# Attention with group norm, 8 images on one core: transposes in one block per tile, or singly between 512-column products

## Chip, cores and metric

One core of a Trainium2 chip runs the whole program. The metric is the time on the device in microseconds, from the start of an execution to its end; the times below are of several executions.

## The reference

Eight images `x` of 128 channels and 32 x 32 places (1024 tokens) go through a group norm, one attention head of width 128 and an output projection, with the input added at the end:

```
h = group_norm(x, gn_w, gn_b)                  # 32 groups of 4 channels
hf = h.reshape(B, C, 1024)
q = einsum('bcn,oc->bno', hf, wq) + bq
k = einsum('bcn,oc->bon', hf, wk) + bk
v = einsum('bcn,oc->bno', hf, wv) + bv
alpha = softmax(einsum('bnc,bcm->bnm', q, k) / sqrt(C), axis=-1)
out = einsum('bnm,bmc->bnc', alpha, v)
out = einsum('bnc,oc->bon', out, wo) + bo
return out.reshape(B, C, 32, 32) + x
```

## The kernel before

The projections of q and k are folded into one matrix (`u = A h`), those of v and of the output into another, so that per image (a batch of the program) there are the logits `u^T h` and the products with v. Each matrix is held as a 16-bit high part and a 16-bit low part, and each product is made of three: high x high, high x low, low x high.

A batch has 8 query tiles of 128 tokens. Each goes through this chain, over all engines:
1. TensorE `logits` (L471, L473, L475): 6 products of 512 columns into `S[n % 2]`, 1024 logits per query.
2. VectorE `tile_max`: the row maximum (L812) and from it the bias of the exponentials (L818).
3. ScalarE `exponentials` (L670): `probs[n % 2]` and the sums of the rows. The instruction that reads the sum stands in the profile as a second one of the same line.
4. TensorE `transposes` (L535): eight 128 x 128 transposes of 32-bit data, four into the bank `pT[0]` (half 0) and four into `pT[1]` (half 1).
5. ScalarE `high_parts` (L682): the 16-bit high part of each half, `pT_hi`.
6. VectorE `low_parts` (L828): the low part of each half, `pT_lo`.
7. TensorE `values` (L498 to L500): products with v over a group of four query tiles (512 columns), 6 per iteration: iterations 4 to 7 do group 0 of the batch, iterations 0 to 3 group 1 of the batch before. The first of a group (k == 0) waits for the low parts of the group and for the bank `O` to be copied out by ScalarE (`copy_values`, L653). `last_values` does the last group of the last batch in two halves.

The order on each engine is written out by hand in that engine's `batch`; semaphores carry the counts between them. In iteration j TensorE does the logits of tile j + 1, a projection in some iterations (`project_u`, three products of 512 columns; `project_v`, products of 129 columns, L416 to L418), the products with v, and the eight transposes of tile j. ScalarE does copies (`copy_u` L634, `copy_v` L644, `copy_values`), both high parts of tile j, then the exponentials of tile j + 1; behind those of tile 3 it adds a logarithm and an exponential for the next batch's group norm (`inverse_deviation`, L658 and L660). VectorE does the maximum and the bias of tile j + 1, in some iterations a piece of the next batch's group norm (`group_spread`, `group_affine`, `normalise`, L804), and both low parts of tile j; in the first iteration and in iteration 5 also the `reciprocals` of the sums (L839, L842), which SP sends to HBM and back as rows (`inv_line`, `inv_rows`). POOL splits h, u and v in parts and makes the output from `av`, the rows and x.

The rules of step 4 are these waits, of which each stands ahead of a first transpose:

```
pe.wait_ge(exp_done, T + 1)
...
    if not first:

        pe.wait_ge(lo_done, 2 * T - 1 + half)
```

Of the kernel before, what the change touches and what calls it, by code (L numbers as in the profile page):

```python
# [5 lines left out]
def groupnorm_attention_kernel(  # L6
# [16 lines left out]

    fp32, fp16 = mybir.dt.float32, mybir.dt.float16  # L40
    ALU = mybir.AluOpType
# [4 lines left out]
    N = HH * WW  # L46
# [9 lines left out]
    VW = C + 1  # L56
    V_PARTS = [(0, 3), (3, 3), (6, 2)]
# [6 lines left out]
    with ctx:  # L64
# [53 lines left out]
        probs = sb("probs", [128, 2, N], fp32)  # L118
# [16 lines left out]

# [278 lines left out]
        def _(pe):  # L414
# [32 lines left out]
            def logits(b, p, n, first):  # L447
# [21 lines left out]
                halves = [slice(c * HALF, (c + 1) * HALF) for c in range(N // HALF)]  # L469
                for c in halves:  # L470
                    nc.tensor.matmul(s[:, c], q_hi, h_hi[:, p, c], start=True, stop=False)  # L471
                for c in halves:
                    nc.tensor.matmul(s[:, c], q_hi, h_lo[:, p, c], start=False, stop=False)  # L473
                for c in halves:
                    last = nc.tensor.matmul(s[:, c], q_lo, h_hi[:, p, c], start=False, stop=True)  # L475
                last.then_inc(qk_done, 1)

            def values(b, j, p, first_group):
# [15 lines left out]
                for m in (2 * k, 2 * k + 1):  # L494
# [3 lines left out]
                    nc.tensor.matmul(O[:, :], vh, ph, start=(m == 0), stop=False)  # L498
                    nc.tensor.matmul(O[:, :], vh, pl, start=False, stop=False)  # L499
                    last = nc.tensor.matmul(O[:, :], vl, ph, start=False, stop=(m == TILES - 1))  # L500
                last.then_inc(av_done, 1)

            def last_values(half, key_tiles):

                bank = (misc, O)[half]
                if key_tiles[0] == 0 and half == 0:

                    pe.wait_ge(v_done, NV * B)
                if key_tiles[0] == 0:

                    pe.wait_ge(lo_done, 2 * (TILES * B - GT // 2 * (1 - half)))
# [3 lines left out]
                for m in key_tiles:  # L515
# [6 lines left out]
                if key_tiles[-1] == TILES - 1:  # L522
                    done.then_inc(last_av, 1)

            def transposes(b, n, first):
                T = TILES * b + n

                pe.wait_ge(exp_done, T + 1)
                for half in range(2):
                    if not first:  # L530

                        pe.wait_ge(lo_done, 2 * T - 1 + half)
                    for t in range(GT):
# [444 lines left out]
```

## Time and profile before

| | |
|---|---|
| median of 3 runs | 269.64 us (269.6 to 270.23) |
| profiled execution, span from first to last instruction | 266.8 us |
| its own time beside the span | not given apart; its median is 2.8 us above the span |
| TensorE (PE) busy | 254.4 us, 95% |
| VectorE (DVE) busy | 220.5 us, 83% |
| ScalarE (ACT) busy | 175.1 us, 66% |
| GpSimd (POOL) busy | 166.3 us, 62% |
| granted TensorE clock | 0.999 of full |

The span is that of one execution, with the launch and the end of the program outside it. Busy time counts instructions at work, and overlapping ones once. A busy TensorE is no TensorE at its peak, since its products are pipelined: how long one holds the array is read from the distance to the next start, and not from its own length. L numbers are lines of the kernel before.

### The profile page before, as it was taken

How to read it: one execution, taken by the hardware profiler on the slowest of the kernel's cores; microseconds unless marked ns; L12 is line 12 of the kernel's file. 1: busy time of each engine (PE TensorE's matmuls, PEld its weight loads, DVE VectorE, ACT ScalarE, POOL GpSimd, SP SyncE). 2: the span in 40 equal slices, each digit the busy share in tenths (PEclk: the TensorE clock that was granted, in tenths of full speed). 3: DMA queues.
4: the chain of work that ended last, by engine and by line, in shares of the span. 5: the costliest groups of instructions: out<-in, count | busy, mean ns of one | idle time of the engine just before them, and what ended most of it. 6: DMA issues, size and time to landing. Idle time of an engine off the chain costs nothing.

```text
span 266.8 us, 4984 instructions
## 1 busy us (share of the span) xinstructions
PE 254.4 (95%) x1599; PEld 157.1 (59%) x1599; DVE 220.5 (83%) x403; ACT 175.1 (66%) x338; POOL 166.3 (62%) x182
## 2 busy tenths in 40 slices
PE   2998999999999999999999999999999999999992
PEld 1655565655566655655665566566656556665581
DVE  2779988999888897988889898988979998678752
ACT  2457766766775786667666866766677677667650
POOL 4056394726978189744979089772997359790621
PEclk9999999999999999999999999999999999999999
DMA  4202004110141102320032102320021200211033
GB/s 118 79 0 81 1 0 119 29 53 2 18 143 40 39 2 40 121 79 0 0 93 103 42 0 40 118 79 0 0 79 17 62 0 5 75 39 42 0 82 115
DMA packets 9806, 13.05 MB, mean 49 GB/s; under 512 B 3904, under 2 KB 4672, under 8 KB 9792
## 3 DMA queue, kind: packets, MB, share of 16 engines
q1 hardware_dynamic: 9504, 12.75, 16.8%
q10 hardware_dynamic: 288, 0.13, 0.2%
q8 instruction: 6, 0.10, 0.2%
q14 instruction: 8, 0.07, 0.1%
HBM read 8.65 MB, written 4.23 MB: 48 GB/s over the span
## 4 chain that ended last, share of the span: by engine, by line
PE 90%; DMA 4%; DVE 3%; ACT 1%; issue 1%; ACTq 0%; POOL 0%; DVEq 0%
PE pT L535 21%; PE S L471 10%; PE S L473 10%; PE S L475 10%; PE O L500 10%; PE O L498 10%; PE O L499 10%; PE misc L417 3%; PE misc L416 3%; PE misc L418 3%; DMA wk_sb<-in_L_conv_wk_dram 1%; DMA inv_rows<-inv_line 1%; DMA inv_line<-row_inv 1%; ACT probs L670 1%; DVE pT_lo L828 1%
## 5 line engine op out<-in xcount | busy, mean ns | idle before, releaser
L828 DVE SCALAR_TENSOR_TENSOR pT_lo<-pT,pT_hi 128x512 f16<-128x512 f32 x128 | 82.8, 683 | 22.3 <-ACT pT_hi L682 22.3
L682 ACT ACTIVATE pT_hi<-pT 128x512 f16<-128x512 f32 x128 | 69.9, 596 | 39.8 <-PE pT L535 39.3
L812 DVE TENSOR_REDUCE neg_max<-S 128x1 f32<-128x1024 f32 x64 | 77.7, 1214 | 1.4 <-PE S L475 0.7
L670 ACT ACTIVATE probs<-S,exp_bias 128x1024 f32<-128x1024 f32 x64 | 71.7, 1121 | 1.8 <-DVE exp_bias L818 1.3
L535 PE MATMUL pT<-ident,probs 128*128 128x128 f32 x512 | 67.4, 274 | 1.8 <-DVE pT_lo L828 1.3
L535 PEld LDWEIGHTS pT<-ident,probs 128*128 128x128 f32 x512 | 58.6, 141 | 14.9 <-ACT probs L670 3.6
L498 PE MATMUL O<-pT_hi,v_hi 128*128 128x512 f16 x120 | 45.5, 379 | 0.0
L499 PE MATMUL O<-pT_lo,v_hi 128*128 128x512 f16 x120 | 45.5, 379 | 0.0
L500 PE MATMUL O<-pT_hi,v_lo 128*128 128x512 f16 x120 | 45.5, 379 | 0.0
L327 POOL TENSOR_TENSOR h_hi<-h,zero 128x512 f16<-128x512 f32 x14 | 14.6, 1041 | 47.8 <-DVE h L804 47.8
L471 PE MATMUL S<-h_hi,u_hi 128*128 128x512 f16 x128 | 38.4, 382 | 0.1
L473 PE MATMUL S<-h_lo,u_hi 128*128 128x512 f16 x128 | 38.1, 379 | 0.0
L475 PE MATMUL S<-h_hi,u_lo 128*128 128x512 f16 x128 | 38.1, 379 | 0.0
L368 POOL TENSOR_TENSOR attn<-av,inv_rows 128x512 f32<-128x512 f32 x15 | 23.2, 1546 | 6.8 <-DMA inv_rows<-inv_line 6.8
L337 POOL TENSOR_TENSOR u_hi<-u,zero 128x512 f16<-128x512 f32 x15 | 15.6, 1041 | 12.4 <-ACT u L634 12.4
L473 PEld LDWEIGHTS S<-h_lo,u_hi 128*128 128x128 f16 x128 | 12.6, 98 | 15.5 <-issue 0.6
L475 PEld LDWEIGHTS S<-h_hi,u_lo 128*128 128x128 f16 x128 | 12.5, 98 | 15.1
L818 DVE TENSOR_SCALAR exp_bias<-neg_max,c_tok 128x1 f32<-128x1 f32 x64 | 17.5, 273 | 4.7 <-POOL c_tok L347 1.9
L355 POOL TENSOR_TENSOR v_lo<-v,v_hi 128x384 f16<-128x384 f32 (+1 forms) x24 | 19.4, 810 | 1.9
L352 POOL TENSOR_TENSOR v_hi<-v,zeros 128x384 f16<-128x384 f32 (+1 forms) x24 | 20.4, 849 | 0.0
L376 POOL TENSOR_TENSOR y<-attn,xres 128x512 f32<-128x512 f32 x15 | 19.0, 1269 | 2.0
L498 PEld LDWEIGHTS O<-pT_hi,v_hi 128*128 128x128 f16 x120 | 11.7, 98 | 14.3 <-DVE pT_lo L828 2.3
(119 smaller groups left out, 318.9 us busy)
## 6 DMA issues: line engine op xcount, KB each, us to landing
inv_rows<-inv_line SPq DMA_DIRECT2D x16, 256.0 KB, 3.8
out_dram<-y SPq DMA_DIRECT2D x15, 256.0 KB, 2.0
x_sb<-in_x_dram SPq DMA_DIRECT2D x7, 512.0 KB, 3.2
x_sb<-in_x_dram SPq DMA_DIRECT2D x2, 256.0 KB, 3.4
inv_line<-row_inv SPq DMA_DIRECT2D x16, 2.0 KB, 1.4
out_dram<-y SPq DMA_DIRECT2D x2, 128.0 KB, 1.9
wq_sb<-in_L_conv_wq_dram ACTq DMA_DIRECT2D x1, 64.0 KB, 3.4
wk_sb<-in_L_conv_wk_dram ACTq DMA_DIRECT2D x1, 64.0 KB, 3.8
```

Of the source, the lines that this page charges most:

```text
L368: nc.gpsimd.tensor_tensor(by_tile(attn[:, q, :]), by_tile(av[:, q, :]), inverses(q), ALU.mult).then_inc(attn_done, 1)
L471: nc.tensor.matmul(s[:, c], q_hi, h_hi[:, p, c], start=True, stop=False)
L473: nc.tensor.matmul(s[:, c], q_hi, h_lo[:, p, c], start=False, stop=False)
L475: last = nc.tensor.matmul(s[:, c], q_lo, h_hi[:, p, c], start=False, stop=True)
L498: nc.tensor.matmul(O[:, :], vh, ph, start=(m == 0), stop=False)
L499: nc.tensor.matmul(O[:, :], vh, pl, start=False, stop=False)
L500: last = nc.tensor.matmul(O[:, :], vl, ph, start=False, stop=(m == TILES - 1))
L535: last = nc.tensor.transpose(pT[half][:, t, :], probs[:, n % 2, m * 128:(m + 1) * 128], ident[:, :])
L670: nc.scalar.activation(probs[:, n % 2, :], S[n % 2][:, :], ACT.Exp, bias=exp_bias[:, p, n:n + 1], accum_out=row_sum[:, p, n:n + 1]).then_i ...
L682: nc.scalar.activation(pT_hi[:, g, half * GT:(half + 1) * GT, n % GT, :], pT[half][:, :, :], ACT.Copy, scale=P_SCALE).then_inc(hi_done, 1)
L812: nc.vector.tensor_reduce(out=neg_max[:, p, n:n + 1], in_=S[n % 2][:, :], axis=AX.X, op=ALU.max, negate=True).then_inc(max_step, 1)
L828: nc.vector.scalar_tensor_tensor(out=pT_lo[:, g, ms, n % GT, :], in0=pT[half][:, :, :], scalar=P_SCALE, in1=pT_hi[:, g, ms, n % GT, :], op ...
```

## The change

TensorE's transposes no longer stand in one block. The four of half 0 of tile j stand one by one behind the first four of the six products with v of iteration j, and the four of half 1 behind the first four of the six logits products of iteration j + 1. In the first batch, where iterations 0 to 3 have no products with v, half 0 stands alone. ScalarE and VectorE follow: iteration j begins with the high and low part of half 1 of tile j - 1 (`past`), and half 0 of tile j comes later; on ScalarE the copies of `O` moved to the start of iterations 0 and 4, and that of u behind the high part. On VectorE the group norm's affine and its first normalisation stand before both low parts. `last_values` runs whole behind all transposes. The buffer `probs` has PB = 2 tiles, as before. The arithmetic is the same.

```diff
-            def logits(b, p, n, first):
+            def transpose_one(tile, half, t):
+
+                b, n, first = tile
+                T = TILES * b + n
+                if t == 0 and half == 0:
+
+                    pe.wait_ge(exp_done, T + 1)
+                if t == 0 and not first:
+
+                    pe.wait_ge(lo_done, 2 * T - 1 + half)
+                m = half * GT + t
+                moved = nc.tensor.transpose(pT[half][:, t, :], probs[:, n % PB, m * 128:(m + 1) * 128],
+                                            ident[:, :])
+                if t == GT - 1:
+                    moved.then_inc(tr_done, 1)
+
+            def logits(b, p, n, first, tile=None):
...
+                for i in range(6):
+                    c = slice(i % 2 * HALF, (i % 2 + 1) * HALF)
+                    last = nc.tensor.matmul(s[:, c], (q_hi, q_hi, q_lo)[i // 2],
+                                            (h_hi, h_lo, h_hi)[i // 2][:, p, c], start=(i < 2), stop=(i >= 4))
+                    if tile and i < GT:
+
+                        transpose_one(tile, 1, i)
                 last.then_inc(qk_done, 1)
...
-            def values(b, j, p, first_group):
+            def values(b, j, p, first_group, tile):
...
+                    if i < GT:
+
+                        transpose_one(tile, 0, i)
                 last.then_inc(av_done, 1)
...
             def batch(b, p, first, last):
 
                 np = 1 - p
                 for j in range(TILES):
+                    tile = (b, j, first and j == 0)
+                    past = (b, j - 1, first and j == 1) if j else (None if first else (b - 1, TILES - 1, False))
                     if j < TILES - 1:
-                        logits(b, p, j + 1, first and j == 0)
+                        logits(b, p, j + 1, first and j == 0, past)
                     elif not last:
-                        logits(b + 1, np, 0, False)
+                        logits(b + 1, np, 0, False, past)
+                    else:
+                        for t in range(GT):
+                            transpose_one(past, 1, t)
...
                     if not first or j >= GT:
-                        values(b, j, p, first and j == GT)
-                    if last and j == TILES - 1:
-                        last_values(0, (0, 1))
+                        values(b, j, p, first and j == GT, tile)
+                    else:
+                        for t in range(GT):
+                            transpose_one(tile, 0, t)
...
-                    transposes(b, j, first and j == 0)
-                    if last and j == TILES - 1:
-                        last_values(0, range(2, TILES))
...
             batch(B - 1, 1, False, True)
-            last_values(1, range(TILES))
+            for t in range(GT):
+                transpose_one((B - 1, TILES - 1, False), 1, t)
+            last_values(0)
+            last_values(1)
...
             def batch(b, p, first, second, last):
                 for j in range(TILES):
-                    if j == 0:
-                        copy_u(b, 1, first)
+                    past = (b, j - 1, not first) if j else (None if first else (b - 1, TILES - 1, False))
+                    if j == 0 and not first:
+                        copy_values(b - 1, 0, second)
+                    if j == 4 and not first:
+                        copy_values(b - 1, 1, second)
+                    if past:
+                        high_part(past, 1)
...
-                    high_parts(b, p, j, not first)
+                    high_part((b, j, not first), 0)
+                    if j == 0:
+                        copy_u(b, 1, first)
+                    if j == 4:
+                        copy_v(b, 2, first)
                     if j < TILES - 1:
-                        exponentials(b, p, j + 1, first and j == 0)
+                        exponentials(b, p, j + 1, first and j + 1 < PB)
...
             def batch(b, p, r, first, second, last):
                 for j in range(TILES):
+                    past = (b, j - 1) if j else (None if first else (b - 1, TILES - 1))
...
+                    if past:
+                        low_part(past, 1)
                     if j < TILES - 1:
                         tile_max(b, p, j + 1)
...
                     if j == 3 and not last:
-                        low_parts(b, j, (0,))
                         group_affine(b + 1, 1 - p)
                         normalise(b + 1, 1 - p, 0)
-                        low_parts(b, j, (1,))
-                    else:
-                        low_parts(b, j)
+                    if j == 4 and not last:
+                        normalise(b + 1, 1 - p, 1)
+                    low_part((b, j), 0)
```

TensorE in iteration 3, before (`S0` and `S1` are the two banks of logits, here those of tile 4; `pT0` and `pT1` are the banks of half 0 and half 1; the products into `O` are those with v):

```order
L471 MATMUL S0<-h_hi,u_hi 128x512
L473 MATMUL S0<-h_lo,u_hi 128x512 x2
L475 MATMUL S0<-h_hi,u_lo 128x512 x2
L498 MATMUL O<-pT_hi,v_hi 128x512
L499 MATMUL O<-pT_lo,v_hi 128x512
L500 MATMUL O<-pT_hi,v_lo 128x512
L498 MATMUL O<-pT_hi,v_hi 128x512
L499 MATMUL O<-pT_lo,v_hi 128x512
L500 MATMUL O<-pT_hi,v_lo 128x512
...
L532 ISA [waits exp_done]
L535 MATMUL pT0<-ident,probs 128x128 [waits lo_done]
L535 MATMUL pT0<-ident,probs 128x128 x3
```

and after, in the same iteration, its end of logits and its products with v:

```order
L441 MATMUL pT1<-ident,probs 128x128
L470 MATMUL S0<-h_hi,u_lo 128x512 x2
L498 MATMUL O<-pT_hi,v_hi 128x512
...
L439 ISA [waits exp_done]
L441 MATMUL pT0<-ident,probs 128x128 [waits lo_done]
L498 MATMUL O<-pT_lo,v_hi 128x512
L441 MATMUL pT0<-ident,probs 128x128
L498 MATMUL O<-pT_hi,v_lo 128x512
L441 MATMUL pT0<-ident,probs 128x128
L498 MATMUL O<-pT_hi,v_hi 128x512
L441 MATMUL pT0<-ident,probs 128x128
L498 MATMUL O<-pT_lo,v_hi 128x512
```

The wait for the tile's exponentials stood behind all six products with v and stands now behind the first of them; half 1 has gone on to the next iteration's logits.

ScalarE, from the exponentials of tile 2 to those of tile 5, before:

```order
L670 ACTIVATE probs,row_sum<-S0,exp_bias 128x1024 [waits tr_done,bias_done]
L682 ACTIVATE pT_hi<-pT0 128x4x128 [waits tr_done]
L682 ACTIVATE pT_hi<-pT1 128x4x128 [waits tr_done]
L670 ACTIVATE probs,row_sum<-S1,exp_bias 128x1024 [waits tr_done,bias_done]
L658 ACTIVATE ln_var<-var_eps 128x1 [waits var_out]
L660 ACTIVATE rstd0<-ln_var 128x1 [waits ln_step]
L653 COPY av<-O 128x512 [waits attn_done,av_done]
L682 ACTIVATE pT_hi<-pT0 128x4x128 [waits tr_done]
L682 ACTIVATE pT_hi<-pT1 128x4x128 [waits tr_done]
L670 ACTIVATE probs,row_sum<-S0,exp_bias 128x1024 [waits tr_done,bias_done]
```

and after:

```order
L663 ACTIVATE probs,row_sum<-S0,exp_bias 128x1024 [waits tr_done,bias_done]
L675 ACTIVATE pT_hi<-pT1 128x4x128 [waits tr_done]
L675 ACTIVATE pT_hi<-pT0 128x4x128 [waits tr_done]
L663 ACTIVATE probs,row_sum<-S1,exp_bias 128x1024 [waits tr_done,bias_done]
L651 ACTIVATE ln_var<-var_eps 128x1 [waits var_out]
L653 ACTIVATE rstd0<-ln_var 128x1 [waits ln_step]
L675 ACTIVATE pT_hi<-pT1 128x4x128 [waits tr_done]
L675 ACTIVATE pT_hi<-pT0 128x4x128 [waits tr_done]
L663 ACTIVATE probs,row_sum<-S0,exp_bias 128x1024 [waits tr_done,bias_done]
L646 COPY av<-O 128x512 [waits attn_done,av_done]
L675 ACTIVATE pT_hi<-pT1 128x4x128 [waits tr_done]
```

The high part of half 1 (`pT1`) of a tile stood ahead of the next tile's exponentials and stands now behind them, and the copy of `O` behind those of tile 4.

VectorE, iteration 3, before:

```order
L812 TENSOR_REDUCE neg_max<-S0 128x1 [waits qk_done]
L818 TENSOR_SCALAR exp_bias<-neg_max,c_tok 128x1 [waits max_step]
L828 SCALAR_TENSOR_TENSOR pT_lo<-pT0,pT_hi 128x4x128 [waits hi_done]
...
L804 TENSOR_SCALAR h<-x_sb,ga,gc 128x512 [waits h_ready,affine]
L828 SCALAR_TENSOR_TENSOR pT_lo<-pT1,pT_hi 128x4x128 [waits hi_done]
L812 TENSOR_REDUCE neg_max<-S1 128x1 [waits qk_done]
```

and after:

```order
L810 TENSOR_REDUCE neg_max<-S0 128x1 [waits qk_done]
L816 TENSOR_SCALAR exp_bias<-neg_max,c_tok 128x1 [waits max_step]
...
L802 TENSOR_SCALAR h<-x_sb,ga,gc 128x512 [waits h_ready,affine]
L826 SCALAR_TENSOR_TENSOR pT_lo<-pT0,pT_hi 128x4x128 [waits hi_done]
L826 SCALAR_TENSOR_TENSOR pT_lo<-pT1,pT_hi 128x4x128 [waits hi_done]
L810 TENSOR_REDUCE neg_max<-S1 128x1 [waits qk_done]
```

The order of low parts and maxima is the same; only the normalisation has moved ahead of the low part of half 0.

## Rows read from the trace of the kernel before

**Rows 1.** The page: busy time and share of each engine, and the chain
```profile
PE 254.4 (95%) x1599; PEld 157.1 (59%) x1599; DVE 220.5 (83%) x403; ACT 175.1 (66%) x338; POOL 166.3 (62%) x182
...
PE 90%; DMA 4%; DVE 3%; ACT 1%; issue 1%; ACTq 0%; POOL 0%; DVEq 0%
```

**Rows 2.** Busy time in the window of one batch (from its header)
```profile
core 0: us, PE busy (x) PEld busy (x) DVE busy (x) ACT busy (x) POOL busy (x), PEclk, DMA share, GB/s
113.34:143.99 30.65, 30.65 (x197) 18.78 (x197) 26.58 (x49) 21.36 (x42) 21.62 (x23) 1.00 0.17 51
```

**Rows 3.** Waits: us in total, times, longest us
```profile
PEld pT L535 <- ACT probs L670: 3.6, 5, 1.1
...
PEld pT L535 <- DVE pT_lo L828: 1.9, 6, 0.5
```

**Rows 4.** Chain by time, steady batch: start us, us held, what
```profile
119.67 0.87 PE pT L535 x8
120.54 0.43 PE S L471 x2
```

**Rows 5.** Timeline of PE (start us, us, instruction), 123.2 to 123.4, 127.2 to 128.3
```profile
123.20 0.22 PE L417 MATMUL misc<-wvc_lo,h_hi 128*128 128x129 f16 x1
123.25 0.22 PE L418 MATMUL misc<-wvc_hi,h_lo 128*128 128x129 f16 x1
123.31 0.28 PE L535 MATMUL pT<-ident,probs 128*128 128x128 f32 x1
...
127.21 0.38 PE L500 MATMUL O<-pT_hi,v_lo 128*128 128x512 f16 x1
127.43 0.27 PE L535 MATMUL pT<-ident,probs 128*128 128x128 f32 x1
...
127.97 0.49 PE L535 MATMUL pT<-ident,probs 128*128 128x128 f32 x3
128.30 0.38 PE L471 MATMUL S<-h_hi,u_hi 128*128 128x512 f16 x1
```

**Rows 6.** Timeline of ACT, 118 to 129 and 254 to 256
```profile
118.60 0.21 ACT L658 ACTIVATE ln_var<-var_eps 128x1 f32<-128x1 f32 x1
118.84 0.20 ACT L660 ACTIVATE rstd<-ln_var 128x1 f32<-128x1 f32 x1
119.71 0.59 ACT L653 COPY av<-O 128x512 f32<-128x512 f32 x1 [0.66 <-PE O L500]
120.19 1.09 ACT L682 ACTIVATE pT_hi<-pT 128x512 f16<-128x512 f32 x2
...
126.41 0.69 ACT L634 ACTIVATE u<-misc,ub 128x512 f32<-128x512 f32 x1
...
128.06 1.09 ACT L682 ACTIVATE pT_hi<-pT 128x512 f16<-128x512 f32 x2 [0.97 <-PE pT L535]
...
254.82 1.12 ACT L670 ACTIVATE probs<-S,exp_bias 128x1024 f32<-128x1024 f32 x1
...
255.91 0.60 ACT L653 COPY av<-O 128x512 f32<-128x512 f32 x1
```

**Rows 7.** Timeline of DVE, 121 to 125 and 128.7
```profile
121.43 0.21 DVE L784 SCALAR_TENSOR_TENSOR newton<-rstd,var_eps 128x1 f32<-128x1 f32 x1
...
122.93 0.68 DVE L828 SCALAR_TENSOR_TENSOR pT_lo<-pT,pT_hi 128x512 f16<-128x512 f32 x1
123.53 1.21 DVE L812 TENSOR_REDUCE neg_max<-S 128x1 f32<-128x1024 f32 x1
124.78 0.27 DVE L818 TENSOR_SCALAR exp_bias<-neg_max,c_tok 128x1 f32<-128x1 f32 x1
...
128.69 0.69 DVE L828 SCALAR_TENSOR_TENSOR pT_lo<-pT,pT_hi 128x512 f16<-128x512 f32 x1 [0.22 <-ACT pT_hi L682]
```

**Rows 8.** Timeline of ACT: exponentials of tiles 0 and 1, and of batches 1 and 7
```profile
16.62 1.11 ACT L670 ACTIVATE probs<-S,exp_bias 128x1024 f32<-128x1024 f32 x1 [0.69 <-DVE exp_bias L818]
...
19.54 1.12 ACT L670 ACTIVATE probs<-S,exp_bias 128x1024 f32<-128x1024 f32 x1
...
44.26 1.13 ACT L670 ACTIVATE probs<-S,exp_bias 128x1024 f32<-128x1024 f32 x1
...
229.12 1.13 ACT L670 ACTIVATE probs<-S,exp_bias 128x1024 f32<-128x1024 f32 x1
```

**Rows 9.** Chain by time at the end of the span
```profile
256.06 0.18 DVE scaled_sum L839
...
256.47 2.48 DMA inv_line<-row_inv
...
258.97 3.45 DMA inv_rows<-inv_line
...
264.04 0.42 DVE y L950
```

**Rows 10.** Groups by line and shape: busy us, mean ns
```profile
L771 DVE SCALAR_TENSOR_TENSOR spread<-dmean,mv 128x1 f32<-128x1 f32 x8 | 6.6, 831 | 0.3
```

More of the change, by code:

```diff
@@ L468, in logits @@
                 s, q_hi, q_lo = S[n % 2], u_hi[:, p, n * 128:(n + 1) * 128], u_lo[:, p, n * 128:(n + 1) * 128]
[L469 to L475, printed above, removed]
+                for i in range(6):
[4 more added lines that the diff above has]
+                        transpose_one(tile, 1, i)
                 last.then_inc(qk_done, 1)
-            def values(b, j, p, first_group):
+            def values(b, j, p, first_group, tile):
                 q, d, g, k = group_of(b, j)
@@ L493, in values @@
                         pe.wait_ge(av_out, g)
-                for m in (2 * k, 2 * k + 1):
+                for i in range(6):
+                    m = 2 * k + i // 3
                     vh, vl = v_hi[:, pv, m, 0:C], v_lo[:, pv, m, 0:C]
@@ L497, in values, with last_values @@
                     pl = pT_lo[:, q, m, :, :].rearrange("p t n -> p (t n)")
-                    nc.tensor.matmul(O[:, :], vh, ph, start=(m == 0), stop=False)
-                    nc.tensor.matmul(O[:, :], vh, pl, start=False, stop=False)
-                    last = nc.tensor.matmul(O[:, :], vl, ph, start=False, stop=(m == TILES - 1))
+                    last = nc.tensor.matmul(O[:, :], (vh, vh, vl)[i % 3], (ph, pl, ph)[i % 3],
+                                            start=(m == 0 and i == 0), stop=(m == TILES - 1 and i == 5))
+                    if i < GT:
+                        transpose_one(tile, 0, i)
                 last.then_inc(av_done, 1)
-            def last_values(half, key_tiles):
+            def last_values(half):
                 bank = (misc, O)[half]
-                if key_tiles[0] == 0 and half == 0:
+                if half == 0:
                     pe.wait_ge(v_done, NV * B)
-                if key_tiles[0] == 0:
-                    pe.wait_ge(lo_done, 2 * (TILES * B - GT // 2 * (1 - half)))
+                    pe.wait_ge(v_out, NV * B)
+                pe.wait_ge(lo_done, 2 * (TILES * B - GT // 2 * (1 - half)))
                 if half == 1:
                     pe.wait_ge(av_out, 2 * B - 1)
-                for m in key_tiles:
+                for m in range(TILES):
                     vh, vl = v_hi[:, 1, m, 0:C], v_lo[:, 1, m, 0:C]
@@ L521, in last_values @@
                     done = nc.tensor.matmul(o, vl, ph, start=False, stop=(m == TILES - 1))
[L522 to L533, printed above, removed]
-                        m = half * GT + t
-                        last = nc.tensor.transpose(pT[half][:, t, :], probs[:, n % 2, m * 128:(m + 1) * 128],
-                                                   ident[:, :])
-                    last.then_inc(tr_done, 1)
+                done.then_inc(last_av, 1)
             def batch(b, p, first, last):
@@ L742, in _ @@
             batch(B - 1, 1, False, False, True)
+            high_part((B - 1, TILES - 1, False), 1)
+            copy_values(B - 1, 0, False)
         @block.vector
@@ L861, in batch @@
                         group_spread(b + 1, 1 - p)
-                    if j == 4 and not last:
-                        normalise(b + 1, 1 - p, 1)
                     if j == 2 and not last:
```

42 lines of the change are left out of this document (19 added, 23 removed).

## Prediction

> **What bounds the kernel now.** I read the page first, then TensorE's rows, then ScalarE's and VectorE's. The page puts TensorE at 95% of the span and at 90% of the chain that ended last; VectorE is busy 83%, ScalarE 66% [rows 1]. In a whole batch of the steady loop, between two neighbouring group means in the chain, TensorE is busy for all of the 30.65 us, VectorE for 26.58, ScalarE for 21.36 [rows 2]. So a batch lasts as long as its products and transposes. The reader should see two things in these rows: TensorE has no slack, and VectorE has only 4 us of it per batch. TensorE waited for ScalarE's exponentials and for the low parts only a few times: 3.6 and 1.9 us in all [rows 3].
>
> **Part 1: what a single transpose costs TensorE.** Before, a tile is six products of logits (0.43 us per two), six products with v, and a block of eight transposes of 0.87 us [rows 4], 0.109 each. After, the same 8 transposes and 12 products stand alternately. The pairs that the new order makes all exist already. Product, then transpose: the first transpose starts 0.216 us after the product before it, as a product after a product does. Transpose, then product: three transposes from 127.97 and the logits' product at 128.30, so the last of them holds the array 0.109 us too, although what follows is a 16-bit product whose weights load fast: behind a 129-column product the next one starts 0.056 us later, and so does even a transpose, with its 32-bit weights [rows 5]. A transpose's own record lasts 0.27 us; one of 129 columns 0.22 and one of 512 columns 0.38, so by length it streams like some 256 columns. I take 0.109 for a single transpose: 0.216 x 12 + 0.109 x 8 = 3.46 us per tile before and after, a gain of 0. The Trainium skill (TensorE: Matmul & The Clock Gate, "LDWEIGHTS (loading the stationary operand)" and "Back-to-back issue gap") says that a load of 128 columns takes 128/1.2 = 107 ns and a 128-column product warm 56 ns. By that the block is bound by its loads, and each single transpose would save some 50 ns, 27 us over 512. The rows speak against it, since the wait behind the last transpose is the same 0.109 with a fast load behind it.
> As a bound from the nearest rows, a single transpose costs between 0.056 (the 129-column product's slot) and 0.109; the other end gives TensorE 512 x 0.053 = 27 us. Part 2 says why little of that would be seen.
>
> **Part 2: ScalarE's new order closes a loop of one tile.** VectorE's order hardly changes: low part of half 0, low part of half 1, row maximum of the tile two further, its bias. ScalarE's does: the high part of half 1 of tile j stood before the exponentials of tile j+1 and stands now behind them. So: exponentials j+1, high part of (j, half 1), low part of it, maximum j+2, bias, exponentials j+2. Each waits for the one before, once per tile, whatever TensorE does. Priced from rows [rows 6, 7]:
> exponentials to the next ScalarE instruction 1.09 (254.82 to the copy at 255.91); high part 0.60 and 0.03 to the low part (128.06 to 128.69); low part to maximum 0.60 (122.93 to 123.53); maximum to bias 1.25 (123.53 to 124.78); bias 0.27; 0.03 to the exponentials. Sum 3.87 us per tile, 30.96 per batch. That alone is above TensorE's 30.65. In the kernel before, both high parts lie ahead of the exponentials, so that the same pieces close only over two tiles, and TensorE's 3.46 to 4.1 us per tile cover them.
>
> **Part 3: what else hangs in that loop**, per batch, on top of 30.96:
> - Iteration 0. The copy of O (group 0 of the batch before) now comes after the exponentials of tile 0: 0.48 to the next instruction (119.71 to 120.19 [rows 6]). The products with v of iteration 0 may only start when it has ended (0.59), at 1.09 + 0.59 + 0.04 = 1.72 after the exponentials started, where TensorE is ready at about 1.05. Then 1.73 for products and transposes, the projection of u behind them (last product 0.43 later, its end 0.39), and ScalarE's copy of u (0.69, of which about 0.59 holds ScalarE) stands ahead of the exponentials of tile 1: 1.72 + 1.73 + 0.43 + 0.39 + 0.02 + 0.59 = 4.88 instead of 3.87: +1.01.
> - Iteration 3. Logarithm and exponential of the deviation stand between exponentials 3 and the high part: about +0.39 (118.60 to the end near 119.0).
> - Iterations 3 and 4. VectorE does the normalisation (1.50 from 121.43 to 122.93 [rows 7]) now before the low part of (3, half 0), and the products with v of iteration 4 wait for that low part, because they open a new group. Low part done 2.1 after exponentials 4 start; TensorE, ready 1.9 earlier, stands. Behind it come 1.73 of products, the second piece of v (0.28 + 0.22), its copy 0.28, then exponentials 5: 2.10 + 1.73 + 0.28 + 0.22 + 0.03 + 0.28 = 4.64: +0.77. The copy of O after exponentials 4 (0.48) lies beside this.
> - Iterations 5 and 6: TensorE is late by 0.04 and 0.10, for the projections.
> Sum 30.96 + 1.01 + 0.39 + 0.77 + 0.14 = 33.27 per batch, against 30.65 to 30.96 now ([rows 8]: 184.86 us for the six from the first exponentials of batch 1 to those of batch 7, 30.81 each). 6 x 2.46 = +14.8.
>
> **First batch, last batch, end.** The first has no products with v in four iterations; its first exponentials come 2.9 us apart (16.62 and 19.54 [rows 8]). Now: 1 waits for the projection of u behind the lone transposes (19.8 instead of 19.5), then 3.87 per tile, 0.39 and 0.77 as above: batch 1 starts at 48.2 instead of 44.26 [rows 8], +3.9. The last batch has no normalisation and no next u or v: 4.88 + 3 x 3.87 + 4.35 (copy of O) + 2 x 3.87 = 28.6 to its last exponentials, before 254.82 - 229.12 = 25.70: +2.9. Behind them the end hangs on the reciprocals, two transfers and VectorE's last four instructions [rows 9]. The reciprocals stood 1.24 after the exponentials' start and now stand behind a high part and a low part: 1.09 + 0.60 + 0.03 + 0.60 = 2.32: +1.1. The last products on TensorE (48 of 256 columns, at 0.109) then end at about the same moment as the second transfer.
> Sum +14.8 + 3.9 + 2.9 + 1.1 = +22.7: span 266.8 to 289.5. The profiled execution's own time is not shown apart; between span and the median of 269.64 lie 2.8 us of start and end, which I keep. **Forecast 292.3 us.**
> The queues: SP and POOL issue the same, in the same order; POOL is busy 21.6 of 30.65 us per batch [rows 2] and gains room as batches get longer. What the last tile loses, products for (0, 1) ahead of its transposes, lies beside the transfers.
>
> **Rivals.**
> A. *The loop holds, but the extra pieces hide* (TensorE's waits are absorbed later, copies slip between). Then a batch is 30.96 plus the 0.48, 0.39 and 0.48 of ScalarE's own pieces, 32.3, and the ends cost half: +9 + 5 = about 284. For it: ScalarE has idle time. Against: each piece is in the loop by its place in the order. If single transposes also cost 0.056, the lengths 1.73 above fall to 1.51 and the two big extras shrink by 0.3 or so each: about 288.
> B. *More waits than counted*: VectorE's spread instruction has a mean of 0.83 us [rows 10] and stands before a low part that TensorE and the next low part wait for; I counted it as hidden. 0.5 to 1 us per batch: 296 to 300.
> C. *Faster, the rule's case.* Single transposes cost 0.056 and the loop turns in less than its rows: TensorE's batch is 30.65 - 3.39 = 27.3 and VectorE's 26.58, so 3.4 x 7.7 = 26 us less, 244. It decides only if the loop with its extras falls below 30.65 a batch, a turn below 3.54 us where the rows give 3.87. Nothing in the rows shortens it.
> D. *No change*: TensorE binds as before and neither side moves it, 270. It needs the turn to be 3.54 too.
>
> **How the numbers follow.** Forecast as priced, with the inner bounds of A and B (284 to 300): 0.80; the loop weaker still, 272 to 284: 0.09; above 300: 0.04; D: 0.03; C: 0.04. The likeliest value is the sum, 292. The range of 8 in 10 is 284 to 300. A measurement of this kernel tells about 0.3% from no change, 0.8 us; faster 0.04, same 0.03, slower 0.93.
>
> **What would show it.** In the changed profile: (1) single transposes with the next product 0.109 us behind (right) or 0.056 (wrong) and TensorE's busy sum per batch; (2) the exponentials 3.87 us apart in iterations 1, 2, 6, 7, with high part, low part, maximum and bias head to tail between them, and batches of about 33.3 us; (3) TensorE idle before the products with v of iterations 0 (0.7 us) and 4 (1.9 us), released by the copy of O and by a low part, and before the first transposes; (4) ScalarE and VectorE in the chain that ended last where TensorE stood with 90%. I would be wrong if the high part of half 1 started long after the exponentials ended, waiting for TensorE, or if batches were still 30.7 us.

## The result, and the profile after

| | before | after |
|---|---|---|
| median, same chip | 269.62 us (268.35 to 270.23) | 294.25 us (293.55 to 295.2) |
| ratio | | 1.0902 (1.0868 to 1.0935) |
| span of the profiled execution | 266.8 us | 291.8 us (its own time 293.55) |

The change costs 24.6 us, 9.0%. The forecast was 292.3 us, the range 284 to 300.

The page of the changed kernel, busy time and the chain that ended last, answers to [rows 1]:

```profile
PE 258.4 (89%) x1599; PEld 170.2 (58%) x1599; DVE 213.6 (73%) x403; ACT 180.3 (62%) x338; POOL 165.9 (57%) x182
...
DVE 31%; ACT 23%; PE 21%; issue 19%; DMA 3%; ACTq 1%; DVEq 0%; POOL 0%
```

TensorE fell from 90% of the chain to 21%. VectorE, ScalarE and "issue" hold most of the rest; in the loop below "issue" is mostly the inside of instructions at work, 0.90 us of the exponentials and 0.56 of the low part. No engine is busier than 89%, and none was added more than 5.2 us of work: the kernel is bound by an order of waits. The window of batch 4, between its first exponentials and those of batch 5, answers to [rows 2] (window; its us; busy time of each engine):

```profile
148.99:182.91 33.92, 31.25 (x196) 20.44 (x195) 26.07 (x50) 22.12 (x41) 21.53 (x23) 1.00 0.15 47
```

This batch takes 33.92 us (the six take 33.73 on the mean, before 30.81) where the window of [rows 2] was 30.65, and TensorE stands for 2.67 of them. The granted clock is the upper level throughout (1.00), so none of this is the clock's. The waits of the changed kernel (us in total, times, longest) answer to [rows 3]:

```profile
ACT probs L663 <- DVE exp_bias L816: 23.6, 34, 1.7
PEld O L498 <- DVE pT_lo L826: 12.0, 6, 2.0
PE O L498 <- DVE pT_lo L826: 10.9, 7, 1.8
...
PEld pT L441 <- ACT probs L663: 8.0, 7, 1.9
...
PE O L498 <- ACT av L646: 6.8, 8, 1.0
```

The exponentials wait for their bias 34 times; before they did so 3 times, for 1.3 us. The products with v wait at a low part six or seven times, with 1.6 to 2.0 us each: once per batch, at iteration 4. They wait at the copy of O once per batch, at iteration 0.

The chain by time (start us, us held, what), one turn of the loop, from the exponentials of tile 2 of batch 4 to those of tile 3:

```profile
157.93 0.04 ACT probs L663
157.97 0.90 issue
...
159.14 0.50 ACT pT_hi L675
...
159.66 0.05 DVE pT_lo L826
159.71 0.56 issue
160.26 1.23 DVE neg_max L810
...
161.61 0.28 DVE exp_bias L816
161.91 0.04 ACT probs L663
```

This is the loop of the prediction, in its order: exponentials, high part, low part, maximum, bias, exponentials, with TensorE nowhere in it. From engine to engine the work goes over within 0.03 us. In this turn 0.12 us instead of 0.03 lie between the maximum and its bias; that term comes back below.

TensorE's timeline of the same batch (start us, us, instruction): the start of the products with v of iteration 0, logits in iteration 1, and the start of iteration 4's products with v:

```profile
150.81 0.38 PE L498 MATMUL O<-pT_hi,v_hi 128*128 128x512 f16 x1 [0.96 <-ACT av L646]
151.05 0.33 PE L441 MATMUL pT<-ident,probs 128*128 128x128 f32 x1
151.21 0.38 PE L498 MATMUL O<-pT_lo,v_hi 128*128 128x512 f16 x1
...
153.26 0.38 PE L470 MATMUL S<-h_hi,u_hi 128*128 128x512 f16 x1
153.48 0.27 PE L441 MATMUL pT<-ident,probs 128*128 128x128 f32 x1
153.59 0.38 PE L470 MATMUL S<-h_hi,u_hi 128*128 128x512 f16 x1
153.80 0.27 PE L441 MATMUL pT<-ident,probs 128*128 128x128 f32 x1
...
166.12 0.59 PE L470 MATMUL S<-h_hi,u_lo 128*128 128x512 f16 x2
168.25 0.39 PE L498 MATMUL O<-pT_hi,v_hi 128*128 128x512 f16 x1 [1.54 <-DVE pT_lo L826]
```

Product to transpose 0.22, transpose to product 0.11: a single transpose holds the array as long as one in a block. In iteration 0 TensorE waited 0.96 us for the copy of O (0.67 to 0.96 over batches 1 to 7). At iteration 4 TensorE stands from about 166.55 (166.12 and two products of 0.216) to 168.25, for a low part.

### The profile page after: what moved, and what is told of

Read it like the earlier page. It is cut to its first block, busy times and chain, and to the rows that moved or that the text cites. A ratio compares the mean times of both kernels' runs of the same rounds, so it can differ in the third digit from the quotient of the medians.

```text
span 291.8 us, 4987 instructions
## 1 busy us (share of the span) xinstructions
PE 258.4 (89%) x1599; PEld 170.2 (58%) x1599; DVE 213.6 (73%) x403; ACT 180.3 (62%) x338; POOL 165.9 (57%) x182
## 4 chain that ended last, share of the span: by engine, by line
DVE 31%; ACT 23%; PE 21%; issue 19%; DMA 3%; ACTq 1%; DVEq 0%; POOL 0%
DVE neg_max L810 19%; ACT probs L663 13%; ACT pT_hi L675 8%; PE O L498 8%; DVE pT_lo L826 5%; DVE exp_bias L816 4%; PE pT L441 4%; PE S L470 3%; ACT av L646 1%; PE misc L401 1%; DMA wk_sb<-in_L_conv_wk_dram 1%; PE misc L399 1%; PE misc L400 1%; DMA inv_rows<-inv_line 1%; DVE h L802 1%
## 5 line engine op out<-in xcount | busy, mean ns | idle before, releaser
L441 PE MATMUL pT<-ident,probs 128*128 128x128 f32 x512 | 137.6, 274 | 6.4 <-ACT probs L663 4.5
L826 DVE SCALAR_TENSOR_TENSOR pT_lo<-pT,pT_hi 128x512 f16<-128x512 f32 x128 | 87.9, 688 | 59.8 <-ACT pT_hi L675 58.3
L675 ACT ACTIVATE pT_hi<-pT 128x512 f16<-128x512 f32 x128 | 76.2, 596 | 59.7 <-PE pT L441 59.6
L441 PEld LDWEIGHTS pT<-ident,probs 128*128 128x128 f32 x512 | 71.2, 140 | 27.1 <-ACT probs L663 8.0
L470 PE MATMUL S<-h_hi,u_hi 128*128 128x512 f16 x128 | 45.3, 382 | 0.1
L470 PE MATMUL S<-h_lo,u_hi 128*128 128x512 f16 x128 | 44.9, 379 | 0.0
L470 PEld LDWEIGHTS S<-h_hi,u_hi 128*128 128x128 f16 x128 | 13.7, 108 | 9.9 <-issue 0.8
```

The source lines that it names most:

```text
L441: moved = nc.tensor.transpose(pT[half][:, t, :], probs[:, n % PB, m * 128:(m + 1) * 128], ident[:, :])
L470: last = nc.tensor.matmul(s[:, c], (q_hi, q_hi, q_lo)[i // 2], (h_hi, h_lo, h_hi)[i // 2][:, p, c], start=(i < 2), stop=(i >= 4))
L675: nc.scalar.activation(pT_hi[:, g, half * GT:(half + 1) * GT, n % GT, :], pT[half][:, :, :], ACT.Copy, scale=P_SCALE).then_inc(hi_done, 1)
L826: nc.vector.scalar_tensor_tensor(out=pT_lo[:, g, ms, n % GT, :], in0=pT[half][:, :, :], scalar=P_SCALE, in1=pT_hi[:, g, ms, n % GT, :], op ...
```

## The experiments

Two questions were open: whether the loop through ScalarE is the cause, and what a single transpose costs when TensorE does bind. Medians of before in the experiments' own jobs lie at 269.75 to 269.92 us; each ratio is to before.

| run | built on | us | ratio, interval | expected |
|---|---|---|---|---|
| e1 | after | 285.69 | 1.0587 (1.0569 to 1.0605) | 279, missed |
| e2 | e1 | 286.07 | 1.0609 (1.0580 to 1.0639) | 273, missed |
| e3 | e2 | 298.97 | 1.1059 (1.1032 to 1.1087) | as e2, missed |
| e4 | before | 292.12 | 1.0820 (1.0802 to 1.0838) | 274, size missed |
| e5 | before | 277.11 | 1.0293 (1.0231 to 1.0355) | 276.6 |
| e6 | before | 282.62 | 1.0481 (1.0418 to 1.0543) | 283.6 |
| e7 | after | 279.64 | 1.0379 (1.0316 to 1.0442) | 278 |
| e8 | before | 269.36 | 1.0001 (0.9967 to 1.0034) | 268.6 |
| e9 | after | 292.08 | 1.0829 (1.0802 to 1.0856) | 292.1 |
| e10 | before | 268.73 | 0.9956 (0.9935 to 0.9977) | 268.8 |
| e11 | e1 | 279.64 | 1.0374 (1.0331 to 1.0416) | 276 |

### e4: ScalarE's new order alone, in the kernel before

```
-                    high_parts(b, p, j, not first)
+                    high_parts(b, p, j, not first, (0,))
...
-                        if j == 2 and not last:
-                            inverse_deviation(b + 1, 1 - p)
+                    high_parts(b, p, j, not first, (1,))
+                    if j == 2 and not last:
+                        inverse_deviation(b + 1, 1 - p)
```

> The kernel before with one edit on ScalarE: the high part of half 1 of tile j stands behind the exponentials of tile j+1, as in the changed kernel, and the logarithm of the deviation behind it. TensorE keeps its block of eight and VectorE its order. Loop theory: the one-tile loop of 3.87 us exists now beside TensorE's 3.46 to 4.1 us per tile; a batch lasts 31.0 (TensorE's long tiles make up for short ones) to 31.9 us (they don't): 274 us (271 to 279). If the loop isn't the cause, it stays at 269.6 within 0.8.

Measured 292.12 us. TensorE's order is that of before, with its block of eight transposes. This one edit on another engine costs 22.2 us, where the whole change costs 24.6. The page (the chain) and the waits of this run:

```profile
DVE 44%; issue 25%; ACT 18%; PE 4%; DMA 3%; POOL 3%; ACTq 1%; DVEq 1%; POOLq 0%
```
```profile
ACT probs L670 <- DVE exp_bias L819: 57.7, 61, 1.5
```

61 of 64 exponentials wait for their bias. In batches 1 and 2 the steps from tile 1 to 2, 2 to 3 and 3 to 4 are 3.89 us each, the turn of the loop. The size was missed because more of VectorE's work sits inside this loop than I had reckoned. Its timeline in iteration 0 of batch 4:

```profile
149.87 1.28 DVE L758 BATCH_NORM_STATS2 bn<-x_sb 128x6 f32<-128x512 f32 x2
151.27 1.22 DVE L813 TENSOR_REDUCE neg_max<-S 128x1 f32<-128x1024 f32 x1
152.53 0.27 DVE L819 TENSOR_SCALAR exp_bias<-neg_max,c_tok 128x1 f32<-128x1 f32 x1
...
154.64 0.69 DVE L829 SCALAR_TENSOR_TENSOR pT_lo<-pT,pT_hi 128x512 f16<-128x512 f32 x1 [0.52 <-ACT pT_hi L682]
155.25 1.21 DVE L813 TENSOR_REDUCE neg_max<-S 128x1 f32<-128x1024 f32 x1
```

Here the channel statistics of the next batch (1.28, and 0.1 to the maximum) lie between the low part and the maximum, while in iteration 1 the maximum follows its low part after 0.61: that step takes 5.2 to 5.4 us. In iteration 6 the reciprocals stand there too (0.3 us), and that step takes 4.3 to 4.5. In batches 3 to 6 nearly every turn is another 0.08 to 0.22 us longer: the exponentials start 0.12 us behind the end of their bias (152.92 in ScalarE's timeline) instead of 0.04, and every third bias 0.1 later behind its maximum; why was not tried. So the loop is shown to be ScalarE's order by itself. That it costs the same in the kernel of the change is not thereby shown: there the statistics run ahead of the low part (149.37 to 150.65, the low part at 151.20) and cost the loop nothing, and it has extras that e4 has not, so that 22.2 and 24.6 lie close in part by chance.

### e1: VectorE takes the maximum ahead of the low part

```
-                    if past:
-                        low_part(past, 1)
                     if j < TILES - 1:
                         tile_max(b, p, j + 1)
...
+                    if past:
+                        low_part(past, 1)
```

> The changed kernel with one edit on VectorE: the maximum and bias of tile j+1 stand before the low part of half 1 of tile j-1, no longer behind it. That opens the one-tile loop (exponentials, high part, low part, maximum, bias), and nothing else moves. Loop theory: batches fall from 33.7 us to TensorE's 30.7 plus two waits per batch, 0.3 us for the copy of O before iteration 0 and about 1.0 for the low part of (3, half 0) behind the normalisation; 279 us (275 to 283). Rival 1, that the placing of the transposes itself costs the time (each single transpose slower, or TensorE losing time at each turn): it stays within 2 us of 294. Rival 2, that the waits for O and for the group's low parts carry most of the loss: it stays above 287.

Measured 285.69 us: 8.6 us less than the change as it stands, where 15 were expected. The low part is out of the loop, and from tile 1 to 2, 2 to 3 and 7 to the next 0 the exponentials now come 3.45, 3.60 and 3.46 us apart. But 3 to 4 takes 3.96 to 4.06, 0 to 1 has grown from 4.92 to 5.13 and more, and 4 to 5 from 4.62 to 4.95 and more. The waits of e1 that have grown, and its timeline of TensorE (one logits group of batch 4) and VectorE:

```profile
PEld pT L441 <- DVE pT_lo L826: 27.4, 51, 2.0
```
```profile
157.39 0.38 PE L470 MATMUL S<-h_hi,u_hi 128*128 128x512 f16 x1
158.00 0.33 PE L441 MATMUL pT<-ident,probs 128*128 128x128 f32 x1 [0.23 <-DVE pT_lo L826]
158.16 0.38 PE L470 MATMUL S<-h_hi,u_hi 128*128 128x512 f16 x1
...
159.14 0.59 PE L470 MATMUL S<-h_hi,u_lo 128*128 128x512 f16 x2
```
```profile
155.72 1.22 DVE L810 TENSOR_REDUCE neg_max<-S 128x1 f32<-128x1024 f32 x1
157.07 0.27 DVE L816 TENSOR_SCALAR exp_bias<-neg_max,c_tok 128x1 f32<-128x1 f32 x1
157.26 0.68 DVE L826 SCALAR_TENSOR_TENSOR pT_lo<-pT,pT_hi 128x512 f16<-128x512 f32 x1
...
159.77 1.22 DVE L810 TENSOR_REDUCE neg_max<-S 128x1 f32<-128x1024 f32 x1 [1.17 <-PE S L470]
```

A second loop of one tile: maximum at 155.72, bias, low part of half 1 until 157.94, the first transpose behind the first logits product at 158.00 (it overwrites what the low part read), the logits' last products from 159.14, and the next maximum at 159.77: 4.05 us. It runs over TensorE and VectorE, and where the first loop takes 3.89 it hardly shows. (0.1 of the 4.05 lies between the maximum and its bias, 1.35 instead of 1.25; without that it is the 3.96 of the other batches.)

### e2: e1, and the normalisation behind the low part of half 0

```
+                    low_part((b, j), 0)
                     if j == 3 and not last:
                         group_affine(b + 1, 1 - p)
                         normalise(b + 1, 1 - p, 0)
                     if j == 4 and not last:
                         normalise(b + 1, 1 - p, 1)
-                    low_part((b, j), 0)
```

> As the run before, and in iterations 3 and 4 VectorE's normalisation stands behind the low part of half 0 instead of before it. Loop theory: the wait before the products with v of iteration 4 goes too, about 1 us for each of seven batches; 273 us (270 to 276), and TensorE is busy again for nearly all of a batch. Had the normalisation hidden anyway, it equals the run before.

Measured 286.07 us, no gain. Tile 4 to 5 became shorter (4.95 to 4.51 us in batches 1 and 2), but 5 to 6 and 6 to 7 grew, 3.90 to 4.14 and 3.97 to 4.40. The normalisation now stands ahead of the next maximum and low part, which are the second loop. Its waits grew with it, from 27.4 to 34.0 us:

```profile
PEld pT L441 <- DVE pT_lo L826: 34.0, 61, 2.0
```

### e11: e1, with half 1's transposes behind the last four logits products

```
-                    if tile and i < GT:
-                        transpose_one(tile, 1, i)
+                    if tile and i >= 6 - GT:
+                        transpose_one(tile, 1, i - 2)
```

> As e1_max_first, but the transposes of half 1 stand behind the last four of the six logits products instead of the first four. e1_max_first came out 7 us above my 279; its trace has TensorE waiting at the first transposes for low parts (27 and 10 us on its two rows) that stand behind the maximum now, a second loop of one tile: logits, maximum, low part of half 1, next logits' first transpose, about 3.96 us per turn. Here that transpose comes 0.43 us later in TensorE's own order, so that the turn is 3.53: if this loop is what held e1_max_first up, 276 us (272 to 281). If it is something else, for instance the time at the turns between products and transposes: 285 to 287.

Measured 279.64 us. The transposes now overwrite the low part's source two products (0.43 us) later in the order, so the products ahead of them need not wait. The step 3 to 4 is 3.60 instead of 3.96, and 0 to 1 is 4.92 instead of 5.13; these steps, and their like in the first and the last batch (1.2 and 1.5 us), are most of the 6 us between e1 and e11. The chain (page) and the wait of e1 in this run:

```profile
PE 76%; DVE 11%; ACT 4%; DMA 4%; issue 3%; ACTq 0%; DVEq 0%; POOL 0%
```
```profile
PEld pT L441 <- DVE pT_lo L826: 9.4, 24, 1.5
```

With two moves, neither of which takes work away, TensorE bounds the kernel again, with 14.6 us of the loss gone. What is left, 31.75 to 32.2 us per batch against 30.65, is in iterations 0 and 4 (4.9 to 5.0 and 4.8 to 5.2 us, before 4.2 and 3.8 to 4.0). No run moves the copy of O, so that its price in iteration 0 is read from the trace alone.

### e3: e2, with the transposes in blocks of four

```
+                if tile:
+                    for t in range(GT):
+                        transpose_one(tile, 1, t)
...
-                    if tile and i < GT:
-                        transpose_one(tile, 1, i)
...
-                    if i < GT:
-                        transpose_one(tile, 0, i)
+                    if i == 0:
+                        for t in range(GT):
+                            transpose_one(tile, 0, t)
```

> As e2_norm_later, but the transposes stand in blocks of four again: half 1 of tile j-1 ahead of the six logits products, half 0 behind the first product with v. This is the price of single against block where TensorE bounds. My reading of the rows (a transpose holds the array 0.109 us wherever it stands): the same time as e2_norm_later within 1 us. The rule (a block bound by its weight loads, a single one costing 0.056): e2_norm_later would be near 250 and this one some 20 us longer than it.

Measured 298.97 us, 13 above e2. It was meant as a test of the price of a single transpose in the changed kernel and is none, because it moved the second loop too: the block ahead of the logits waits for the low part with all six products queued behind it.

```profile
DVE neg_max L810 <- PE S L473: 56.8, 57, 1.5
```

57 of 64 maxima wait for logits, and the plain step becomes 4.24 us. The rest of the price question went to e5 and e6, where TensorE binds.

### e5 and e6: one or two more transposes between two products, in the kernel before

```
-                for c in halves:
-                    nc.tensor.matmul(s[:, c], q_hi, h_hi[:, p, c], start=True, stop=False)
+                nc.tensor.matmul(s[:, halves[0]], q_hi, h_hi[:, p, halves[0]], start=True, stop=False)
+                for _ in range(1):
+                    nc.tensor.transpose(s[:, HALF:HALF + 128], ident[:, :], ident[:, :])
+                nc.tensor.matmul(s[:, halves[1]], q_hi, h_hi[:, p, halves[1]], start=True, stop=False)
```

e6 has two in place of one. The second product overwrites their columns.

> The kernel before, in which TensorE bounds, with one transpose more per tile: of the identity, alone between the first and second logits product, into columns that the second product overwrites. It is added 64 times and nothing waits for it, so that the time added is 64 times what a single transpose costs between two 512-column products. My reading (0.109 us): +7.0, 276.6 us (275.8 to 277.4). The rule (0.056, load hidden behind the product): +3.6, 273.2 us.

> As the run before, with two such transposes back to back in the same place. By my reading a second one costs what the first does, 0.109: +14.0, 283.6 us (282.6 to 284.6). By the rule the second is bound by its load, 0.107, and the first costs 0.056: +10.4, 280.0 us.

Measured 277.11 and 282.62 us against 269.81, +7.3 and +12.8 us by the medians. TensorE's timeline of e5 and of e6:

```profile
151.73 0.38 PE L470 MATMUL S<-h_hi,u_hi 128*128 128x512 f16 x1
151.94 0.27 PE L472 MATMUL S<-ident 128*128 128x128 f32 x1
152.05 0.38 PE L473 MATMUL S<-h_hi,u_hi 128*128 128x512 f16 x1
```
```profile
151.92 0.38 PE L472 MATMUL S<-ident 128*128 128x128 f32 x2
152.14 0.38 PE L473 MATMUL S<-h_hi,u_hi 128*128 128x512 f16 x1
```

One holds the array for 0.11, two for 0.22. The windows agree: a batch of e5 with TensorE busy throughout is 31.51 us,

```profile
108.61:140.12 31.51, 31.51 (x204) 19.96 (x203) 26.49 (x50) 21.34 (x42) 21.47 (x23) 1.00 0.17 51
```

0.86 above 30.65, 0.108 for each of eight; 64 of them make 6.9 of the 7.3 us. In e6 five of the six batches take 32.39 or 32.40 us between their first exponentials, 1.75 above 30.65, 0.109 for each of sixteen, which makes 14.0. A median that rose by 12.8 only, at the low edge of what I expected, fits the profiles: one of the six batches is a long one in e6 (32.49), where before has three of 30.96 to 30.99, of which the last section tells. A single transpose costs what one in a block costs, and the change had nothing to win from its alternation.

### e7 and e8: half the row maximum, after and before

```
-    P_SCALE = 4096.0
+    P_SCALE = 1.0
...
-                nc.vector.tensor_reduce(out=neg_max[:, p, n:n + 1], in_=S[n % 2][:, :], axis=AX.X, op=ALU.max,
+                nc.vector.tensor_reduce(out=neg_max[:, p, n:n + 1], in_=S[n % 2][:, 0:HALF], axis=AX.X, op=ALU.max,
```

> The changed kernel with VectorE's row maximum over the first 512 of 1024 columns and a scale of 1 in place of 4096; the second half of the maximum is left out. It shortens one link of the one-tile loop by some 0.53 us (1.21 to 0.68) on an engine that is busy 73% of the span. Loop theory: 3.89 falls to 3.36 us, below TensorE's 3.46 per tile, and what stays are the waits before the products of iterations 0 and 4; 278 us (274 to 283). Were the loss in TensorE's own single transposes, or in the waits for O, it would stay above 290.

> The control: the kernel before with the same maximum over half the columns and the same scale; the second half of the maximum is left out. TensorE bounds there and VectorE's work lies beside it: 268.6 us (267.8 to 269.8), against a fall of more than 10 us that the same edit gives in the changed kernel.

Measured 279.64 and 269.36 us. Before, a maximum shorter by half is worth nothing (1.0001, 0.9967 to 1.0034): VectorE is covered. After, it is worth 14.6 us, and the chain goes back to TensorE by half:

```profile
PE 54%; DVE 16%; ACT 14%; issue 11%; DMA 3%; ACTq 0%; DVEq 0%; POOL 0%
```

That VectorE's maximum is in the loop of the one kernel and not of the other is what tells the two apart. From tile 1 to tile 4 steps of 3.45 to 3.74 us take the place of 3.88 to 4.22; the steps 0 to 1 and 4 to 5 stay as they were.

### e9: the change, with the normalisation behind the low part of half 0

The edit of e2, made on the changed kernel instead of on e1.

> The changed kernel with VectorE's normalisation in iterations 3 and 4 behind the low part of half 0 instead of before it, the maximum where the change has it. It prices the term of iterations 3 and 4 by itself: the products with v of iteration 4 then wait only for the copy of O, and the step from exponentials 4 to 5 falls from 4.6 or 4.7 to 4.35 us, some 0.3 us for seven batches: 292.1 us against 294.2 (291.2 to 293.2). If that wait was absorbed elsewhere: 294.

Measured 292.08 us, 2.2 less than the change. The step from tile 4 to 5 goes from 4.58 to 4.76 us down to 4.41 to 4.48; the others of batches 1 to 6 stay within 0.02 us on the mean, and the first batch is 0.8 us shorter. While the first loop sets the pace, nothing else hangs on the normalisation, unlike in e2.

### e10: the kernel before, with the group's spread behind both low parts

```
-                    if j == 1 and not last:
-                        group_spread(b + 1, 1 - p)
...
+                    if j == 1 and not last:
+                        group_spread(b + 1, 1 - p)
```

> The kernel before with the group spread of iteration 1 (mean 0.83 us on VectorE) behind both low parts. In three batches of the trace of before TensorE waited 0.3 us for a low part there. If those waits go: 268.8 us, 0.9 less (268.2 to 269.6). If it only moves them: the same within 0.3 us.

Measured 268.73 us, ratio 0.9956 (0.9935 to 0.9977). Before, batches 1, 4 and 6 lasted 30.96 to 30.99 us and the others 30.65; now all six last 30.65. The spread instruction of [rows 10] is short here (groups by shape: busy us, mean ns):

```profile
L771 DVE SCALAR_TENSOR_TENSOR spread<-dmean,mv 128x1 f32<-128x1 f32 x8 | 2.9, 368 | 0.3
```

0.37 us instead of 0.83. It is the one version whose interval lies below 1, by 0.4%.

## Why the prediction was right

**Part 1, the price of a transpose.** Right, 0.109 in the changed kernel and, where it matters, in e5 and e6. The Trainium skill (TensorE: Matmul & The Clock Gate, "Back-to-back issue gap") gives 56 ns for a 128-column product by itself and some 81 ns in a stream with its loads; it has no figure for a 32-bit transpose. Taken for a single transpose these figures make 64 x 0.056 = 3.6 or 64 x 0.081 = 5.2 us in e5, an estimate. The trace disagrees with both: the transpose holds the array 0.11 us between long products too, and 64 of them cost 7.3 us by the medians (6.2 to 9.6 by the interval of the ratio). TensorE's busy sum rose all the same, from 254.4 to 258.4 us: ahead of a wait the record of the last product runs to its end (0.38 us) and not only to the next start (0.216), as at iteration 4, where a stand of 1.70 us has 1.54 of idle time.

**Part 2, the loop.** Forecast 3.87 us a tile; measured 3.884 to 3.891 in batches 1 and 2 and in the last one. e4 shows that ScalarE's order closes it, e1 and e11 that it opens again when the low part leaves it, and e7 that it gives way when the maximum shrinks.

**Part 3, the extras.** Steps between the exponentials in batch 1, and the range over batches 1 to 6:

| step | forecast | batch 1 | batches 1 to 6 |
|---|---|---|---|
| tile 0 to 1 | 4.88 | 4.92 | 4.92 to 5.06 |
| 1 to 2 | 3.87 | 3.89 | 3.88 to 3.89 |
| 2 to 3 | 3.87 | 3.89 | 3.89 to 3.99 |
| 3 to 4 | 4.26 | 4.22 | 4.21 to 4.22 |
| 4 to 5 | 4.64 | 4.62 | 4.58 to 4.76 |
| 5 to 6 | 3.91 | 3.90 | 3.90 to 3.99 |
| 6 to 7 | 3.97 | 4.03 | 3.89 to 4.04 |
| 7 to next 0 | 3.87 | 3.98 | 3.97 to 4.17 |
| sum | 33.27 | 33.44 | mean 33.73 |

The mechanisms stand: in iteration 0 TensorE waits for the copy of O (0.67 to 0.96 us, 0.7 forecast), and iteration 4 stands from 166.55 to 168.25, 1.7 us (1.9 forecast). The mis-sized terms are small. After the wait in iteration 0 of batch 4 TensorE's first steps are longer, 0.24 and 0.16 instead of 0.216 and 0.109 (behind its other long waits 0.22 to 0.23 and 0.11 to 0.15), so that the 1.73 of six products and four transposes became 1.81, and its product starts 0.15 and not 0.04 behind the copy's end (150.66). The term left out lies in the steps 2 to 3, 5 to 6 and 7 to next 0: in batches 3 to 6 they last 3.98 to 3.99, 3.98 to 3.99 and 4.15 to 4.17 us. All three hold a maximum (of tiles 3, 6 and 0) whose bias also waits for a new piece of c_tok; in the loop above the bias starts 1.35 us behind the maximum (160.26 to 161.61) and not 1.25. Batches 3 to 6 stand in the program's own loops of ScalarE and VectorE (TensorE's loop also holds 1 and 2) and the others don't. That this wait costs 0.1 more there is a reading of these rows; it was not tried. The rest of the step 7 to next 0 has two pieces: the high part of half 1 starts 1.17 us behind the exponentials and not 1.09 (179.92 after 178.75; in batches 1 and 2 too, whose step is 3.97), and in batches 3 to 6 the exponentials of tile 0 start 0.13 us behind the end of their bias and not 0.03. Why they do is open.

**First and last batch, end.** Batch 1 starts at 48.23 (forecast 48.2). The last batch's exponentials span 28.8 (28.6). From the last exponentials to the end it is 12.4 us, where 13.1 was forecast. The chain's end answers to [rows 9]:

```profile
281.75 0.17 DVE scaled_sum L837
...
282.15 1.90 DMA inv_line<-row_inv
...
284.07 3.33 DMA inv_rows<-inv_line
```

The reciprocals start 2.33 us behind the exponentials at 279.42, as priced (2.32). The transfers took 1.90 and 3.33 instead of 2.48 and 3.45: 0.7 us less, which no term held and no run explains.

**The sum.** Span 289.5 forecast, 291.8 measured: +2.8 for six batches at 33.73 instead of 33.27, +0.2 in the last, -0.7 at the end. Span and time lay 1.75 us apart in this execution and 1.7 to 1.8 in the other three, and not 2.8, which took 1.05 back. The 2.8 was no time of start and end alone: the spans of before in the experiments' jobs run from 265.9 to 269.0 us, so that the profiled one, 266.8, was a short one. The batches alone would have made 295; that 292.3 lies nearer to 294.25 is luck, since errors of opposite sign met.

**The rivals.** A (extras hide) fell: each extra is in its step. B (more waits, by the spread) fell as a mechanism: behind the first batch the spread takes 0.48 to 0.50 us in the changed kernel, and the step of its iteration is 3.89. The 0.46 us per batch that came on top have other causes, named above. C and D needed a turn below 3.54 us.

**Where my expectations behind the result failed**, they failed alike: they held too little of the path. For e1 and e2 I followed one loop, took a piece out of it and read the time off TensorE's busy sum. The second loop, low part to transposes to logits to maximum, was 0.1 us longer than the one I had opened, and e11 showed it by moving four transposes by two products. In e4 I counted the loop and not what else VectorE does inside it.

## What to carry to other kernels

When an instruction moves behind another on an engine that is not the bottleneck, follow what it feeds until you come back to the instruction it was moved behind, and add the pieces. If that takes one iteration and its sum is above what the busiest engine needs (here 3.87 against 3.46 us a tile), the loop is the new bound, however idle every engine looks. When you open such a loop, add up the next one before you name the gain.

## What the runs showed that I had not expected

- One edit on ScalarE, at 66% busy, with every instruction the same, costs 22 us of 270 (e4). In the page it appears as "issue" and as short waits and in no busy share.
- A 32-bit transpose of 128 columns holds TensorE's array for 0.11 us at the full clock, singly or in a row (e5, e6), and a 16-bit product of 129 columns for 0.056 [rows 5].
- VectorE's spread instruction, one column wide, takes 1.59 to 1.63 us in batches 1, 4 and 6 of the kernel before and 0.22 in 2, 3 and 5; the first three last 0.32 us longer. Moved by two instructions it takes 0.37 on the mean and the batches are equal (e10). In the three long cases GpSimd's product `attn` starts 0.05 us behind it, and both end within 0.03 us of each other. VectorE and GpSimd before, batch 4:

```profile
144.40 1.59 DVE L771 SCALAR_TENSOR_TENSOR spread<-dmean,mv 128x1 f32<-128x1 f32 x1
144.45 1.53 POOL L368 TENSOR_TENSOR attn<-av,inv_rows 128x512 f32<-128x512 f32 x1
```

In e10 the spread starts while `attn` runs and ends with it (54.08 to 54.40, and 52.86 to 54.38). So it seems to be held until GpSimd's instruction is done. That is a reading of rows, and it leaves a question: in batch 2 `attn` starts 0.05 us behind the spread too, and there the spread is short (0.22) and `attn` long (1.58). No run takes `attn` away to try it.
